# Experts' rows transposed by DMA instead of by TensorE, and four banks for the down projection

## The reference

```python
h = _layernorm(x, axis=-1) * (1 + ca) + sa
x = x + ga * _L0_attn_ref(h, theta_K, theta_V, theta_Q, W0, b0)
h = _layernorm(x, axis=-1) * (1 + cb) + sb
# _L0_ffn_ref(h, ...):
scores = softmax(xf @ router_w); topk_scores, topk_idx = top_k(scores, 2)
combine = zeros((N, E)).at[arange(N)[:, None], topk_idx].add(topk_scores)
y = silu(xf @ gate_w[e]) * (xf @ up_w[e]) @ down_w[e]       # for each expert e
routed = einsum('enh,ne->nh', y, combine)
shared = silu(xf @ shared_gate_w) * (xf @ shared_up_w) @ shared_down_w
x = x + gb * (shared + routed)
```

## Time and profile before

| | |
|---|---|
| median of 3 runs | 1727.09 us |
| profiled execution | 1723.9 us, span of its slowest core (core 0) 1722.3 us |
| spans of the eight cores | 1722.3, 1707.7, 1720.8, 1712.7, 1716.8, 1712.7, 1718.4, 1710.8 us |
| TensorE busy, core 0 | 1537.2 us, 89% of the span |
| VectorE, ScalarE, GpSimd busy | 46%, 30%, 19% of the span |
| the eight expert blocks' gate and up | start at 1110.0, 1157.5, 1208.4, 1259.5, 1310.6, 1361.7, 1412.8 and 1463.8 us |

### The profile page before, as it was taken

How to read it: one execution, slowest core, us unless ns; L and a number is a source line. 1 busy time by engine, 2 the same in 40 slices (tenths; PEclk the granted TensorE clock), 3 DMA queues, 4 the chain that set the end, 5 groups by cost and what they waited for, 6 DMA issues and landing times.

```text
span 1722.3 us, 25790 instructions; the slowest of 8 cores (1707.7 to 1722.3 us)
## 1 busy us (share of the span) xinstructions
PE 1537.2 (89%) x9204; PEld 833.1 (48%) x9204; DVE 789.0 (46%) x1350; ACT 516.7 (30%) x804; POOL 323.9 (19%) x225
## 2 busy tenths in 40 slices
PE   0476989797999998999998899999999999999798
PEld 0233444343454454544443444566776666744343
DVE  2426465646447546654654343332222222223667
ACT  1144454343454434444442311222111111111000
POOL 1048888403300000000101200000000000002221
PEclk9989999898999999999998999999999999999899
DMA  7964333698112122221376295569999999947654
GB/s 179 254 124 131 93 119 111 230 340 286 47 38 62 44 91 86 74 74 62 79 154 184 74 223 172 117 182 197 181 199 198 200 198 184 177 105 242 231 183 159
DMA packets 91542, 262.09 MB, mean 152 GB/s; under 512 B 8083, under 2 KB 8211, under 8 KB 90388
## 3 DMA queue, kind: packets, MB, share of 16 engines
q0 software_dynamic: 55600, 145.25, 38.7%
q1 hardware_dynamic: 30948, 105.68, 18.2%
q10 hardware_dynamic: 4864, 9.44, 2.1%
HBM read 239.92 MB, written 89.65 MB: 191 GB/s over the span
## 4 chain that ended last, share of the span: by engine, by line
PE 75%; DVE 9%; DMA 8%; issue 5%; ACT 1%; POOL 1%; SPq 0%; DVEq 0%; ACTq 0%; POOLq 0%
PE u L834 9%; PE prep L571 9%; PE gate L804 7%; PE up L804 7%; PE prep L834 5%; PE u L733 5%; PE up L799 4%; PE gate L799 4%; PE up L636 3%; PE up L663 3%; PE gate L636 3%; PE gate L653 2%; DMA xb<-xp 2%; DMA ygb<-yx,sl 2%; PE up L698 2%
## 5 line engine op out<-in xcount | busy, mean ns | idle before, releaser
L1191 DVE TENSOR_TENSOR WT<-WT,u 128x512 f32<-128x512 f32 x240 | 153.3, 679 | 46.1 <-PE u L733 45.7
L733 PE MATMUL u<-Gsb,Ktk 128*128 128x512 bf16 x480 | 128.7, 392 | 48.9 <-DVE WT L1191 47.6
L1315 DVE TENSOR_TENSOR act<-up,sgb 128x576 bf16<-128x576 f32 x64 | 48.5, 758 | 199.3 <-PE up L804 199.3
L571 PE MATMUL prep<-hft,s_thK 128*128 128x512 bf16 x512 | 122.3, 387 | 8.5 <-DVE s_thK L1102 3.8
L962 ACT CAST Wbf<-WT 128x1024 bf16<-128x1024 f32 x120 | 124.6, 1040 | 15.8 <-DVE WT L1191 15.7
L1511 POOL DMA_INDIRECT hx<-h2m,sl x32 | 35.0, 1095 | 446.2 <-DVE sl L1295 438.9
L995 ACT ACTIVATE sgb<-gate 128x512 bf16<-128x512 f32 x64 | 38.2, 597 | 256.4 <-PE gate L799 246.9
L997 ACT ACTIVATE sgb<-gate 128x576 bf16<-128x576 f32 x64 | 41.7, 651 | 231.3 <-PE gate L804 231.3
L1312 DVE TENSOR_TENSOR act<-up,sgb 128x512 bf16<-128x512 f32 x64 | 44.2, 690 | 130.4 <-PE up L799 109.2
L834 PE MATMUL u<-w1d,act 128*128 128x512 bf16 (+1 forms) x376 | 89.8, 390 | 14.2 <-DVE tmpy L1325 14.2
L733 PEld LDWEIGHTS u<-Gsb,Ktk 128*128 128x128 bf16 x480 | 44.0, 100 | 106.8 <-issue 69.5
(11 more groups left out here) (247 smaller groups left out, 2701.3 us busy)
## 6 DMA issues: line engine op xcount, KB each, us to landing
hx<-h2m POOLq DMA_DIRECT2D x8, 4096.0 KB, 47.1
x2b<-wmod POOLq DMA_DIRECT2D x32, 512.0 KB, 4.2
yx<-ring SPq DMA_DIRECT2D x32, 512.0 KB, 6.5
xb<-xp SPq DMA_DIRECT2D x16, 512.0 KB
wmb<-wmod SPq DMA_DIRECT2D x8, 1024.0 KB, 9.3
xb<-xm SPq DMA_DIRECT2D x16, 512.0 KB
x2b<-xm SPq DMA_DIRECT2D x16, 512.0 KB, 4.3
x2s<-x2b SPq DMA_DIRECT2D x16, 512.0 KB, 5.3
```

Source lines behind the costliest of these rows:

```text
L571: m = t.matmul(b[:, 0:512], w[:, dt * D + et * P:dt * D + (et + 1) * P], hft[j % 2][:, dt * 512:dt * 512 + 512], start=(dt == 0), stop=(dt ...
L733: m = t.matmul(U[jh][:, 0:512], Ktk[s % 2][:, cc * D + dt * P:cc * D + (dt + 1) * P], Gsb[:, cc * D + jh * 512:cc * D + (jh + 1) * 512], s ...
L1191: v.tensor_add(w, w, U[jh][:, 0:512]).then_inc(S["v_W"], 1)
L1315: v.tensor_mul(ap(act[k % 2], fj * CAP, [[DT * CAP, P], [HC, 2], [1, HC]]), ap(up2, 0, [[1024, P], [512, 2], [1, HC]]), ap(sgb[n % 2], 0, ...
```

## The change

The rows are no longer loaded as they are. SyncE issues one transposing DMA for each expert (`load_rows` in `sync_moe`), which reads 576 x 1024 values of hx and writes them as 128 x 8 x 576 to one of two operand buffers, hfe0 and hfe1. The first two are issued behind the first four loads of x2s; that of expert e+2 is issued once gate and up of expert e are computed, and it stands in SyncE's queue ahead of the five stores of expert e, behind those of expert e-1. TensorE's transposes, ScalarE's copies and ScalarE's loads are gone, and `gate_up` waits for the DMA instead. hxb is gone; the two PSUM banks that the transposes used stay unused, and the bank A[1], free in this part, becomes the fourth bank of the down projection: half q waits for half q-4.

```diff
-        bkT = At[1]
-        Y = (U[0], U[1], A[0])
+        Y = (U[0], U[1], A[0], A[1])
-                hfe = ectx.enter_context(nc.sbuf_tensor("hfe", [P, DT * CAP], BF16))
-                hxb = ectx.enter_context(nc.sbuf_tensor("hxb", [P, TEW * D], BF16))
+                hfe = [ectx.enter_context(nc.sbuf_tensor(f"hfe{i}", [P, DT * CAP], BF16)) for i in range(2)]
...
                 if kind == "e":
-                    t.wait_ge(a_xT, TEW * (i + 1))
+                    t.wait_ge(ld_hx[i % 2], 16 * (i // 2 + 1))
...
-            def expert_rows(k, r):
-                e = BLK[k][1]
-                if r == 0:
-                    t.wait_ge(ld_hx, 32 * (e + 1))
-                if e or r:
-                    t.wait_ge(a_xT, TEW * e + r)
-                w = rows_of(r)
-                for i in range(DT):
-                    m = t.transpose(bkT[:, i * P:i * P + w], hxb[0:w, r * D + i * P:r * D + (i + 1) * P],
-                                    s_ident[0:w, 0:w])
-                m.then_inc(p_xT, 1)
...
-                    if q >= 3:
-                        t.wait_ge(v_y, q - 2)
+                    if q >= 4:
+                        t.wait_ge(v_y, q - 3)
...
-                    if k + 2 < NB and BLK[k + 2][0] == "e" and h in T_AFTER:
-                        expert_rows(k + 2, T_AFTER.index(h))
...
-                if k + 1 < NB and BLK[k + 1][0] == "e":
-                    e = BLK[k + 1][1]
-                    for r in range(TEW):
-                        w = rows_of(r)
-                        s_.wait_ge(p_xT, TEW * e + r + 1)
-                        s_.copy(ap(hfe, r * P, [[DT * CAP, P], [CAP, DT], [1, w]]),
-                                ap(bkT, 0, [[1024, P], [P, DT], [1, w]])).then_inc(a_xT, 1)
-                    if e + 1 < NE:
-                        load_rows(e + 1)
...
+            def load_rows(e):
+
+                sy.dma_start_transpose(ap(hfe[e % 2], 0, [[DT * CAP, P], [CAP, DT], [1, CAP]]),
+                                       ap(d_hx, e * CAP * D, [[D, CAP], [1, D]])).then_inc(ld_hx[e % 2], 16)
...
             for n in range(RING):
                 load_x2(n)
+            for e in range(2):
+                load_rows(e)
...
             for e in range(NE):
+                if e + 2 < NE:
+                    sy.wait_ge(p_u2, DT * (FIRST[1 + e] + 1))
+                    load_rows(e + 2)
                 for r in range(TEW):
```

More of the change, by code:

```diff
@@ L321, in build_program @@
         st_out = sem("st_out")
-        p_xT, p_g2, p_u2, p_y = (sem("p_" + n) for n in ("xT", "gate", "up", "y"))
-        a_own, a_c, a_init, a_W0, a_xT, a_g2 = (sem("a_" + n) for n in ("own", "c", "init", "W0", "xT", "gate"))
+        p_g2, p_u2, p_y = (sem("p_" + n) for n in ("gate", "up", "y"))
+        a_own, a_c, a_init, a_W0, a_g2 = (sem("a_" + n) for n in ("own", "c", "init", "W0", "gate"))
         v_own, v_mod, v_flag, v_act, v_y, v_x3, v_z, v_out = (sem("v_" + n) for n in (
@@ L803, in gate_up @@
                             o = ht * CAP + half * HC
-                            m = t.matmul(banks[half][:, 0:HC], q, hfe[:, o:o + HC],
+                            m = t.matmul(banks[half][:, 0:HC], q, hfe[i % 2][:, o:o + HC],
                                          start=(ht == 0), stop=(ht == DT - 1))
@@ L844, in beyond @@
                 t.wait_ge(v_y, Y0[12])
-                t.wait_ge(a_xT, TEW * NE)
                 for e, j in OVER:
                     x, rows = OVER.index((e, j)), over_rows(j)
-                    t.wait_ge(o_hx, 32 * (x + 1))
-                    for r in range(4):
-                        w = min(P, rows - r * P)
-                        if x or r:
-                            t.wait_ge(o_hf, 4 * x + r)
-                        for i in range(DT):
-                            m = t.transpose(bkT[:, i * P:i * P + w], hxb[0:w, r * D + i * P:r * D + (i + 1) * P],
-                                            s_ident[0:w, 0:w])
-                        m.then_inc(o_xT, 1)
-                    t.wait_ge(o_hf, 4 * x + 4)
+                    t.wait_ge(o_hx, 16 * (x + 1))
                     t.wait_ge(o_w, 48 * (e + 1))
@@ L865, in beyond @@
                                 m = t.matmul(b[:, 0:rows], w[:, ht * D + fj * P:ht * D + (fj + 1) * P],
-                                             hfe[:, ht * CAP:ht * CAP + rows], start=(ht == 0), stop=(ht == DT - 1))
+                                             hfe[0][:, ht * CAP:ht * CAP + rows], start=(ht == 0), stop=(ht == DT - 1))
                             m.then_inc(done, 1)
@@ L1021, in beyond @@
                     rows = over_rows(OVER[x][1])
-                    for r in range(4):
-                        w = min(P, rows - r * P)
-                        s_.wait_ge(o_xT, 4 * x + r + 1)
-                        s_.copy(ap(hfe, r * P, [[DT * CAP, P], [CAP, DT], [1, w]]),
-                                ap(bkT, 0, [[1024, P], [P, DT], [1, w]])).then_inc(o_hf, 1)
                     for fj in range(DT):
@@ L1662, in beyond @@
             def beyond():
-                sy.wait_ge(p_xT, TEW * NE)
+                sy.wait_ge(p_u2, DT * 13)
                 for e, j in OVER:
```

37 lines of the change are left out of this document (10 added, 27 removed).

## The result

The changed kernel takes 1736.56 us (median of 20 runs), the kernel before 1726.20 us (20 runs, same chip). The ratio is 1.0058, 95% interval 1.0041 to 1.0074. The forecast was 1716, faster. The profiled execution took 1731.88 us; spans of the cores 1730.3, 1703.6, 1721.6, 1714.8, 1721.1, 1715.5, 1718.3 and 1711.8 us. Some executions of every kernel, the kernel before too, run several per cent longer at a lower granted clock on some cores: the medians here contain them, the ratios leave them out, and of the profiled executions only that of x_tail4 is such a one.

The account below looks back on a forecast made before the run. TensorE was taken to bound the kernel, with DMA engines just as full in the expert blocks. 18.6 + 1.7 - 9.3 = 11.0 us off 1723.9 gives 1712.9; the median, 3.2 higher, 1716; 8-in-10 range 1703 to 1786.

Parts of the forecast that it names:

- TensorE's saving: Expert blocks: without transposes each expert takes 2.33 us less on TensorE, 18.6 us for eight, all on the path.
- The fourth bank: Down projection behind the experts: two TensorE waits for an empty bank shorten, 0 to 3.5 us, taken as 1.7.
- T: Time of all 16 DMA engines for one transposing load of 576 x 1024 values: taken as 5.8 us, bounds 4.4 to 33.
- The row of 20 ns: Small packets at the program's start, mostly under 512 B, 20 ns each; used as the price of a 256 B piece.
- even: Rival: T between 7.7 and 10.9 us, TensorE's saving goes into waits for weights; about 1726 us, chance 0.14.
- Where the load lies: Expert blocks: load shares engines with the weights, up matrix late by T - 2.7 (3.1 us) every second block; 9.3 us lost.
- X + 48.8: X is the start of an expert's gate and up; 48.8 us later the next expert's weights and rows are needed.
- Late and punctual blocks: Expert blocks: a late start doesn't repeat in the next block, so three of six blocks lose 3.1 us each.
- SyncE blocked: Rival: issuing two transposing loads holds SyncE's queue 69 us in the shared blocks, VectorE stalls 22 us; 1738 us, chance 0.07.

Follow-up runs that it names:

- x_tail4: The kernel before with four banks for the down projection only from the last four blocks on, where the transposes are over; ratio to before 0.9925.
- x_light_after: The changed kernel with weight loads cut to an eighth in six of the eight experts; ratio to before 0.9922.
- x_ahead: The changed kernel with GpSimd waiting for the transposed rows to land before it issues a block's weights; ratio to before 1.0112.
- x_half: The changed kernel with weights loaded in packets of 1 KB in place of 2 KB, same bytes; ratio to before 1.0065.
- x_half_order: x_order_after with weights loaded in packets of 1 KB in place of 2 KB; ratio to before 0.9954, in a repeat 0.9960.
- x_plain: The changed kernel with two plain loads of 2 KB and 1 KB pieces for each transposing one, transposition left out; ratio to before 0.9908.
- x_small: The changed kernel with one plain load, meant to run in 256 B pieces, for each transposing one, transposition left out; ratio to before 1.0142.
- x_early: The changed kernel with yx stores issued by ScalarE and the transposing load issued some 17 us earlier; 1813.2 us, ratio to before 1.0427.
- x_order_after: The changed kernel with the next unit's gate and up weights issued ahead of the down matrix, some 17 us earlier; ratio to before 1.0308.

## Why the prediction was wrong

**TensorE's saving: right.** Forecast 2.33 us an expert; 2.24 in x_light_after, 17.4 us for ten halves.

**The fourth bank: too small.** 1.7 us in the sum (0 to 3.5), 4.6 to 5.5 measured. On core 0 the waits of 14.2 and 1.3 us became one of 6.0, where I had counted one half of 1.75 us for each of two waits and taken half of that. Why one bank more saves more than a half for each wait isn't shown.

**T: too small beside weights.** The pieces are 256 B and 4608, but one took 32 ns in the changed kernel's blocks, so T = 4608 x 32 / 16 = 9.2 us and not 5.8. The row of 20 ns was of packets with a few bytes and nothing large beside them. For a load by itself it is a fair price (18 ns in the median in x_ahead and x_light_after), but not beside weight packets. By my own formulas T = 9.2 gives 3 x 6.5 = 19.5 us lost against 20.3 won: the rival "even", 1726. From 27 ns a piece on (T = 7.7) I would have forecast no gain.

**Where the load lies: this is the step that failed.** The prediction had the load "flow perhaps 1 us before they do" and then share the engines, with the up matrix late by T - 2.7. Sharing was taken as by time. It goes by turns, one piece of 256 B for one weight packet of 2 KB, and with 288 pieces against 192 packets the small load ends behind the big one. So what TensorE waits for is the rows, 12 to 22 us a core, and never the up matrix, and SyncE is held nearly as long (shown by the packet counts, by x_light_after and x_ahead, where the same load lands in 15 and 11 us, and by x_half and x_half_order). The sentence that the load "lands long before X + 48.8 unless T is above some 25 us" is the same error. Late and punctual blocks do alternate from the third on: on core 0 the weights are issued 52.7, 57.9, 48.9, 60.1 and 48.9 us apart.

**SyncE blocked: seen by half.** I priced its queue by issue work for each piece (34.6 us a load). In the expert blocks it is held 41 to 49 us beside weights and 5 to 13 in x_ahead and x_light_after, so it follows the transfer. Where the rival placed the stall, in the shared blocks, the first two loads did hold SyncE from 987.11 to 1040.86 us, 54 us of the 69 forecast, but VectorE waited 7.0 us in all for ring's reloads (4.3 before), not 22; in the expert blocks, where I had called it harmless, it holds back the stores and the next load. That this rival's 1738 lies within 2 us of the measured 1736.6 is luck: it is made of a stall that did not occur.

**The clock: not in the prediction.** Core 0's stretch is 406.2 = 369.5 (x_light_after) + 25.4 (waits) + 11.3, and TensorE is busy for just these 11.3 us more, 380.8 us. The groups behind a wait run at 1.2 GHz for a while (3.55 and 4.00 us for 2.07); it happens five times on core 0, four times behind a wait for rows and once behind the wait of 3.1 us for VectorE. A third of the 36.7 us between the two kernels is this.

**Mean and slowest.** Lost in the stretch: 11.2 us in the mean of the cores; won outside it 5.3 and 4.1, the bank and expert 0's transposes (2.3) among them. In the two profiled executions the mean core lost 1.8 us and the slowest 8, with spans spread over 27 us in place of 15. That the spread is the change's doing isn't shown: over the executions that the ratio counts it is 25 us in the mean for the changed kernel, but the kernel before has 18.5 to 28 us in the sets of the experiments. What is shown is that the stretch, 385 to 386 us on every core before, became 389 to 406.

## What to carry to other kernels

When two queues flow at once, count packets as well as bytes: a load of many small pieces beside a stream of large packets lands when it has had its turns, and may end last though it is the smaller. Compare its pieces for each engine with the other queue's packets in that time. To start it when the other queue is empty, or to cut the other into more packets, cures its lateness, but neither made this kernel faster by itself (1.0112 and 1.0065): the engines' work then falls on the other stream, so ask first whether that has slack. Behind a transposing DMA put nothing in the issuing queue that must leave soon, and price a wait of TensorE with the slow products that follow it.

## What the runs showed of the hardware

- A transposing DMA of 576 x 1024 bf16 values moves in 4608 pieces of 256 B. Its time from issue to landing was 7.3 us at the least and 50.0 in the median beside weights. The Trainium skill ("Advanced Engine Details and Errata", section "X-Bar Transpose (TRN2)") has transposing DMAs as fast as regular ones; here the plain load of the same rows in x_plain landed after 18 us where the transposing one took 50. That is a matter of turns beside weights: by themselves its pieces took 18 ns in the median (x_ahead), 4608 x 18 / 16 = 5.2 us of all engines, against 4.4 for the plain load.
- The issue of it holds the engine's queue until some 1200 to 1600 of its 4608 pieces are left to start (1204 to 1624 in the changed kernel's blocks on core 0, 1192 to 1281 in x_half's). Where the rest goes fast that is almost the whole time, 46.71 of 49.48 us; in x_half it is 29.4 of 43.
- The plain loads of the same bytes held it 2.0 us (x_plain) and 0.7 us (x_small, 1152 packets in all, fewer than those 1200). In the shared blocks, where two were issued back to back, the two held it 28.9 us in x_small, so a plain load can hold it too.
- An engine gave one piece of 256 B for each weight packet, of 2 KB or 1 KB, in turns of 180 ns and, in x_half, 105 ns: 288 turns are 52 and 30 us.
- A piece took 31 ns in the median beside 2 KB or 1 KB packets and 18 ns beside little else (x_light_after). In two kernels with another order of issue the mean was 92 ns (x_early, core 1) and 110 ns (x_order_after, core 5); why is open.
- A plain pattern written in pieces of 256 B went out in packets of 1024 B.
- After an idle time of 3.1 us TensorE's next 16 products took 3.55 us, and after 6.8 us 4.00, in place of 2.07, at a granted clock of 0.57 and 0.50.
